# Six of sixteen gamma kv additions on VectorE, an identity run on TensorE ahead of the data, and a new hand-written order, in a gated recurrent layer kernel on one core

## The reference, cut to what matters

```python
xn = layernorm(x)
r, k, v = split(xn @ W_rkv + b_rkv)          # 128 wide each
r = sigmoid(r); k = exp(k); kv = k * v
# two scans over time, y[t] = lam * y[t-1] + u[t], lam = exp(-exp(nu_log)) per feature
u1 = scan(kv); u2 = scan(k)
gamma = exp(nu_log + gamma_log) - 1
s = ((u1 + gamma * kv) / (u2 + gamma * k + 1e-6) * r) @ W_o + b_o
# weights and xn are quantised in blocks of 32 to a 6 bit grid and back: xd, wd
g = silu(xd @ wd.T + bias)
out = x + s * g
```

## Time and profile before

| what | us |
|---|---|
| median of 3 runs | 125.94 (125.5 to 125.95) |
| the profiled execution, device time | 125.42 |
| its span in the trace | 123.6 |
| TensorE busy in the span | 109.6 (89%) |
| GpSimd busy | 106.4 (86%) |
| VectorE busy | 105.1 (85%) |
| ScalarE busy | 104.7 (85%) |
| TensorE weight loads, beside the matmuls | 58.5 (47%) |

### The profile page before, as it was taken

One profiled execution on the slowest core, in us unless ns is written; L12 is line 12 of the kernel. 1 busy time (PEld: TensorE's weight loads), 2 busy tenths in 40 slices (PEclk: granted clock), 3 DMA queues, 4 the chain that ended last, 5 costly groups with the idle time before them and its releaser, 6 DMA issues.

```text
span 123.6 us, 1670 instructions
## 1 busy us (share of the span) xinstructions
PE 109.6 (89%) x387; PEld 58.5 (47%) x387; DVE 105.1 (85%) x167; ACT 104.7 (85%) x180; POOL 106.4 (86%) x127
## 2 busy tenths in 40 slices
PE   0008989999999999999999999999999999999980
PEld 0006444444555555555455555544654655554450
DVE  0446999999998999999999948998969989993881
ACT  4047799999999999999969899999999979999800
POOL 2288699999997999999999999999999999998400
PEclk9999999999999999999999999999999999999999
DMA  2879930000020000110201020200102002012026
GB/s 66 248 237 402 386 127 0 0 3 0 0 90 5 0 0 26 59 58 27 85 0 65 25 85 0 85 0 3 72 15 90 0 3 85 31 54 85 0 85 255
DMA packets 6025, 8.82 MB, mean 71 GB/s; under 512 B 1536, under 2 KB 1920, under 8 KB 6016
## 3 DMA queue, kind: packets, MB, share of 16 engines
q1 hardware_dynamic: 5040, 8.72, 19.4%
q10 hardware_dynamic: 976, 0.00, 0.4%
HBM read 4.53 MB, written 4.19 MB: 71 GB/s over the span
## 4 chain that ended last, share of the span: by engine, by line
POOL 39%; ACT 17%; PE 16%; issue 12%; DVE 9%; DMA 3%; ACTq 1%; DVEq 1%; POOLq 0%
POOL den L302 8%; POOL mixed L308 7%; PE taken_ps L946 6%; POOL rstd L256 6%; POOL q L279 6%; ACT L679 4%; POOL xd L286 4%; PE v_ps L968 4%; POOL gk L296 3%; ACT den L744 3%; DMA x_all<-in_L_attn_inputs_dram 3%; PE turned_ps L925 3%; POOL xn L271 2%; ACT gate L739 2%; DVE kv L451 2%
## 5 line engine op out<-in xcount | busy, mean ns | idle before, releaser
L946 PE MATMUL taken_ps<-xnT,wrkv_sb 128*128 128x512 f32 x64 | 33.0, 611 | 0.3 <-ACT recept L731 0.3
L696 ACT ACTIVATE xn<-x_all,shift,rstd 128x128 f32<-128x128 f32 x48 | 19.8, 486 | 6.4 <-POOL shift L260 6.4
L308 POOL TENSOR_TENSOR mixed<-mixed,den 128x512 f32<-128x512 f32 x16 | 20.3, 1277 | 1.8 <-DVE mixed L478 1.7
L679 ACT ACT_TABLE_LOAD x16 | 20.5, 1283 | 1.0 <-PEq L1170 0.7
L302 POOL TENSOR_TENSOR den<-den,gk 128x512 f32<-128x512 f32 x16 | 20.4, 1279 | 1.0 <-DVE den L460 0.8
L469 DVE TENSOR_TENSOR_SCAN num_ps<-own_ps,kv 128x512 f32<-128x512 f32 x16 | 19.5, 1217 | 0.2
L460 DVE TENSOR_TENSOR_SCAN den<-own_ps,k 128x512 f32<-128x512 f32 x16 | 19.2, 1204 | 0.3 <-POOL mixed L308 0.3
L925 PE MATMUL turned_ps<-ident,xn 128*128 128x128 f32 x64 | 10.4, 292 | 9.6 <-POOL xn L271 9.6
L422 DVE BATCH_NORM_STATS2 stats<-x_all 128x6 f32<-128x256 f32 x32 | 11.8, 415 | 7.3 <-DMA x_all<-in_L_attn_inputs_dram 7.3
L279 POOL TENSOR_TENSOR q<-xn,inv_scale 128x512 fp8e4<-128x512 f32 x16 | 16.8, 1053 | 1.1 <-DVE inv_scale L443 1.1
L968 PE MATMUL v_ps<-xnT,wrkv_sb 128*128 128x512 f32 x32 | 17.2, 619 | 0.0
(11 more groups left out here) (62 smaller groups left out, 181.0 us busy)
## 6 DMA issues: line engine op xcount, KB each, us to landing
x_all<-in_L_attn_inputs_dram SPq DMA_DIRECT2D x16, 256.0 KB, 6.6
out_dram<-x_all SPq DMA_DIRECT2D x16, 256.0 KB, 2.0
wrkv_sb<-in_L_attn_W_rkv_dram SPq DMA_DIRECT2D x1, 192.0 KB, 4.4
wf_sb<-in_L_ffn_weight_dram SPq DMA_DIRECT2D x1, 64.0 KB, 6.4
wo_sb<-in_L_attn_W_o_dram SPq DMA_DIRECT2D x1, 64.0 KB, 6.1
cols<-in_L_attn_nu_log_dram ACTq DMA_DIRECT2D x1, 0.5 KB, 3.9
cols<-in_L_attn_gamma_log_dram ACTq DMA_DIRECT2D x1, 0.5 KB, 4.2
cols<-in_L_attn_b_o_dram ACTq DMA_DIRECT2D x1, 0.5 KB, 4.6
```

Of the source, the lines that this page charges most:

```text
L308: nc.gpsimd.tensor_tensor(mixed[:, n % MIX, :], mixed[:, n % MIX, :], den[:, n % DEN, :], ALU.mult)\
L679: act.add_instruction(mybir.InstLoadActFuncSet(name=nc.get_next_instruction_name(), engine=mybir.EngineType.Activation, act_func_set_id=n, ...
L696: ins = nc.scalar.activation(xn[:, n % XN, j * D:(j + 1) * D], x_all[:, n, j * D:(j + 1) * D], ACT.Identity, bias=shift[:, t:t + 1], scale ...
L946: nc.tensor.matmul(taken_ps[i % 2][:, :], weights, moving, start=True, stop=True).then_inc(filled, 1)
```

## The change

It has three parts.

1. For sequences 2, 5, 7, 9, 11 and 13, `gamma_kv(n)` goes from TensorE's list to VectorE's. There it is one SCALAR_TENSOR_TENSOR, num = kv * gamma + num, that reads and writes `num_ps`. The other ten stay on TensorE, `arm_num` too.
2. TensorE begins with `warm_up()`: 32 transposes of the identity into `v_ps`, which wait for the identity alone.
3. The lists of calls of GpSimd, VectorE, ScalarE and TensorE, and `TURNS` and `TAKEN` with them, stand in a new order. ScalarE has seven calls each of `exp_phase` and `silu_phase` in place of eight. SyncE's order of loads and stores is as before. GpSimd's calls are the same 103, in another order.

```diff
+    WARM_UP = 32
...
     TURNS = [
-        ("xn", 0), ("xn", 1), ("xn", 2), ("xn", 3), ("xd", 0), ("xd", 1), ("xn", 4), ("xn", 5), ("xn", 6),
+        ("xn", 0), ("xn", 1), ("xn", 2), ("xn", 3), ("xn", 4), ("xd", 0), ("xd", 1), ("xd", 2), ("xn", 5),
...
     TAKEN = [
-        ("k", 0), ("k", 1), ("r", 0), ("r", 1), ("k", 2), ("k", 3), ("r", 2), ("z", 0), ("r", 3), ("z", 1),
+        ("k", 0), ("k", 1), ("r", 0), ("r", 1), ("r", 2), ("k", 2), ("k", 3), ("k", 4), ("z", 0), ("r", 3),
...
             def scan_num(n):
                 if n == 0:
+                    dve.wait_ge(lam_placed, 1)
                     dve.wait_ge(num_armed, 1)
...
+            def gamma_kv(n):
+
+                dve.wait_ge(num_scanned, n + 1)
+                nc.vector.scalar_tensor_tensor(num_ps[:, :], kv[:, n % KS, :], gam[:, 0:1], num_ps[:, :],
+                                               ALU.mult, ALU.add).then_inc(num_done, 1)
...
+            def warm_up():
+
+                pe.wait_ge(ident_ready, 1)
+                for i in range(WARM_UP):
+                    nc.tensor.transpose(v_ps[:, 0:P], ident[:, :], ident[:, :])
...
+            warm_up()
             transpose_xn(0)
             transpose_xn(1)
             keys(0)
+            keys(1)
             values(0)
             arm_num()
-            keys(1)
```

More of the change, by code:

```diff
@@ L352, in _ @@
[L352 to L356, removed]
+            quantise(5)
+            denominator(4)
+            quantise(6)
+            normalise(9)
+            normalise(10)
+            quantise(7)
+            gamma_k(5)
+            dequantise(5)
+            gamma_k(6)
+            ratio(3)
+            inv_std(5)
+            normalise(11)
             dequantise(6)
-            normalise(10)
+            gamma_k(7)
@@ L563, in _ @@
+            scan_num(1)
+            statistics(9)
             scan_den(2)
-            scan_num(2)
             key_values(3)
-            statistics(9)
+            receive(1)
+            scan_den(3)
+            block_maxima(3)
+            statistics(10)
+            statistics(11)
+            statistics(12)
             gating(0)
-            receive(2)
-            block_maxima(3)
-            residual(0)
             block_scales(3)
             inverse_scales(3)
-            statistics(10)
+            key_values(4)
@@ L574, in _ @@
+            scan_num(2)
+            residual(0)
+            gamma_kv(2)
+            scan_den(4)
+            receive(2)
+            gating(1)
+            statistics(13)
             scan_num(3)
-            scan_den(3)
-            key_values(4)
+            residual(1)
+            block_maxima(4)
+            key_values(5)
             receive(3)
-            scan_num(4)
-            key_values(5)
-            statistics(11)
-            statistics(12)
-            block_maxima(4)
-            receive(4)
@@ L584, in _ @@
-            gating(1)
             block_scales(4)
             inverse_scales(4)
-            scan_num(5)
-            residual(1)
-            key_values(6)
-            statistics(13)
-            scan_den(4)
-            gating(2)
-            block_maxima(5)
-            scan_den(5)
-            residual(2)
+            scan_den(5)
+            scan_num(4)
+            gating(2)
+            statistics(14)
+            key_values(6)
+            residual(2)
+            receive(4)
+            statistics(15)
@@ L596, in _ @@
+            block_maxima(5)
+            scan_num(5)
+            block_scales(5)
+            inverse_scales(5)
+            gamma_kv(5)
+            key_values(7)
+            receive(5)
+            gating(3)
             scan_den(6)
-            receive(5)
-            statistics(14)
-            gating(3)
-            key_values(7)
             scan_num(6)
+            scan_den(7)
+            block_maxima(6)
             residual(3)
             key_values(8)
-            block_scales(5)
@@ L605, in _ @@
-            inverse_scales(5)
-            statistics(15)
-            receive(6)
-            scan_den(7)
-            gating(4)
-            scan_num(7)
-            key_values(9)
-            residual(4)
-            scan_den(8)
-            receive(7)
-            block_maxima(6)
-            gating(5)
-            scan_num(8)
             block_scales(6)
             inverse_scales(6)
-            residual(5)
-            gating(6)
-            receive(8)
-            key_values(10)
-            scan_num(9)
@@ L625, in _ @@
-            residual(6)
+            receive(6)
+            scan_num(7)
+            gamma_kv(7)
+            key_values(9)
+            receive(7)
+            gating(4)
+            scan_num(8)
+            residual(4)
+            key_values(10)
+            scan_den(8)
+            receive(8)
+            gating(5)
+            scan_num(9)
+            key_values(11)
+            residual(5)
+            gamma_kv(9)
             scan_den(9)
             receive(9)
+            gating(6)
             scan_num(10)
+            scan_den(10)
@@ L869, in _ @@
[L869 to L886 removed]
+            normalise(13)
+            copy_xdT(8)
@@ new lines, in _ @@
+            receptance(10)
+            normalise(14)
+            gates(7)
+            copy_xnT(12)
+            receptance(11)
+            copy_xnT(13)
+            receptance(12)
+            gates(8)
+            exp_phase()
+            logarithm(8)
+            logarithm(9)
+            keys(12)
+            keys(13)
+            logarithm(10)
+            inverse(8)
+            inverse(9)
+            copy_xdT(9)
+            inverse(10)
+            copy_xdT(10)
+            normalise(15)
@@ L910, in _ @@
             gates(13)
             exp_phase()
+            logarithm(14)
+            copy_xdT(15)
+            inverse(13)
+            inverse(14)
             logarithm(15)
```

443 lines of the change are left out of this document (201 added, 242 removed), and 14 rows, old and new, of tables (TAKEN, TURNS).

## The result

| | before | after |
|---|---|---|
| median us of 4 runs each, same chip | 125.72 (125.1 to 125.95) | 121.67 (121.62 to 121.83) |
| ratio, 95% interval | | 0.969 (0.965 to 0.973) |
| profiled execution, us | 125.42 | 121.62 |
| its span | 123.6 | 119.8 |
| first `quantise` starts | 13.53 | 12.51 |

The change is faster by 3.1%. The forecast was 123.9 with a range from 122.5: the direction was right and the size was not. Against the profiled execution it said -2.0 us; it is -3.8.

What follows compares the result with a forecast made beforehand. GpSimd was taken as the bound: start -0.7, waits that go -2.5, tail -0.2, new waits +1.0 and +0.4 gave -2.0, so 123.4 against the profiled 125.42; plus 0.5 for the runs' median, 123.9, range 122.5 to 125.7 plus 0.2.

Steps and rivals of the forecast that it cites:

- start of GpSimd's stretch: First `quantise`, behind VectorE's first reciprocal: starts at 12.86 in place of 13.53, -0.7 us.
- waits that go: GpSimd's waits ahead of the last `ratio` (1.69 us) and `denominator(3)` (0.85) vanish in the new order, -2.5 us.
- tail: Two ScalarE table loads fewer: the last `project` no longer waits 0.20 for the last `gates`, -0.2 us.
- Waits that come: +1.0 us found: `quantise(2)` on GpSimd: ready at 24.8 but waits for VectorE's third reciprocal, ending at 25.8, +1.0 us.
- +0.4 us assumed: GpSimd, middle of its stretch: small new waits not visible in the lists, +0.4 us, ends 0 and 2.2.
- rival 4: Lighter TensorE and ScalarE free everyone: no wait at `quantise(2)` or in the middle, -1.4 more, 122.5; chance 0.15.
- rival 2: New order gives back on GpSimd what it takes: new middle waits reach 2.2, +1.8, 125.7, no change; chance 0.14.
- TensorE: 5.2 us less, not on the path: Six products leave TensorE, 0.86 us each; nothing on GpSimd's list waits for TensorE directly, only VectorE's waits shorten.
- The warm up, worth 0: TensorE's start: early clock could bring `key_values(0)` forward, but VectorE's queue holds it to 15.3; 0 to 0.3 us, chosen 0.
- rival 3: TensorE's clock falls back while idling before data; `key_values(0)` and passes behind it come 0.6 later, up to 124.5; chance 0.15.
- just hidden: VectorE's six new passes, 0.66 us each, 4.0 in all, cost nothing if it idles at most 2.6 us before `receive(15)`.
- the -1.69: Last `ratio` on GpSimd: its 1.69 us wait for `receive(15)` goes because `receive(15)` and `gating(12)` change places.

Runs made afterwards that it cites:

- The 126.06: Changed kernel with the six gamma kv additions put back on TensorE, so all sixteen there, new order and warm up kept: 126.06 us, ratio 1.004.
- the 125.69: Changed kernel, additions left on VectorE, with six other TensorE products (receptance 5 and 8, keys 11, project 6, 8, 10) made twice: 125.69 us, ratio 1.001.
- the early `ffn_weights()`: Changed kernel without the warm up and with `ffn_weights()` moved ahead of `key_values(0)`: 122.11 us, ratio 0.971; with the warm up kept: 121.74, 0.969.

## Why the prediction was wrong in size

By its own steps, against the profiled 125.42:

| step | said | measured |
|---|---|---|
| start of GpSimd's stretch | -0.7 | -1.0 |
| waits that go | -2.5 | -2.5 |
| waits that come | +1.4 | -0.4 |
| tail | -0.2 | +0.2 |
| sum | -2.0 | -3.8 |
| median of the runs above the profiled execution | +0.5 | 0.05 |

(The third row is what is left of the -2.9 of GpSimd's stretch: 0.25 us fewer small waits, the rest in GpSimd's own passes. The measured rows add up to -3.8 before rounding.)

The last row is chance. The median of three stood 0.5 above the one execution that was profiled, and it makes up 0.45 of the 2.2 us between 123.9 and 121.67.

- **"Waits that come: +1.0 us found"** is the step that failed. It put the third reciprocal at 25.8; it ended at 24.35. It took VectorE's passes ahead of it to have the durations that they had before, and looked only at which of them were moved. But the five passes of `ffn_weights` took 1.3 us (17.71 to 19.00) in place of 2.45 (15.80 to 18.25), since they now stand beside the inverse square root. The rows that would have told it stood in the trace of before. VectorE in order of time:

```profile
16.11 0.62 DVE L515 TENSOR_SCALAR wscale<-wmax 128x4 f32<-128x4 f32 x1
...
17.31 1.02 DVE L523 TENSOR_TENSOR wd<-wq,wscale 128x128 f32<-128x128 fp8e4 x1
```

  and GpSimd beside it:

```profile
15.66 1.05 POOL L279 TENSOR_TENSOR q<-xn,inv_scale 128x512 fp8e4<-128x512 f32 x1
16.69 0.45 POOL L271 TENSOR_SCALAR xn<-x_all,rstd,shift 128x128 f32<-128x128 f32 x1
```

  `wscale`, 128 x 4 numbers, took 0.62 us and ended at 16.73, `quantise` at 16.71. `wos_sb` gave 0.4 back (0.44 before, 0.83 now, where it ends with a `dequantise`: 23.19 and 23.12). The remaining 0.7 of the 1.45 is partly that the fifth input tile landed 0.28 earlier (10.04 against 10.32); I have not taken it apart further.
- **"+0.4 us assumed"** for small waits in the middle: GpSimd's small waits are 1.1 us in all, where those that were not to go had been 2.21 - 0.85 = 1.36. The lighter TensorE is needed to keep new ones away, as the run with six products made twice shows. That is half of rival 4. Its other half, no wait at `quantise(2)`, came true by another cause: with TensorE's load back, `quantise(2)` does not wait either (24.90, behind a reciprocal that ends at 24.82). Rival 4 had 0.15 where it should have had most of rival 2's chance too.
- **"TensorE: 5.2 us less, not on the path"** was wrong as reasoning, though it had no number in the sum. Its record count tells what the busy time of 99.74 of 100.40 did not: 354 matmul records are 185 halves of products, at 0.43 us each by the earlier trace rows, and 169 transposes at 0.11 to 0.12 from one start to the next (four from 106.77 to the product at 107.20 in the changed kernel): 98 to 100 us of 100.4. After, 332 records, 167 and 165 of them: 90 to 92 of 95.4. TensorE was as full as GpSimd. With the six products, 12 halves or 5.2 us, it would have 95 to 97 of 95.4: the new list of GpSimd could not have been fed by it without a wait. The 126.06 and the 125.69 are what that cost at the places tried. "Nothing on GpSimd's list waits for TensorE directly" is not so in the program either, though no such wait shows.
- **"The warm up, worth 0"**: its speed was called rightly (`key_values(0)` at 14.96 against a forecast of 15.3, `values(0)` at 1.02 in place of 1.74), its worth not: 1.0 us (122.64 against 121.67). The 0.6 by which `key_values(0)` would be late was seen, under rival 3, but the other 0.7, VectorE's passes slipping under GpSimd's, was not; and without that slip the 0.6 costs nothing in GpSimd's stretch, as the early `ffn_weights()` shows. The cap that the Trainium skill sets (TensorE: Matmul & The Clock Gate, Part 1: below 1% of a typical span) holds with 0.8%, at its edge. In the old order the warm up gained nothing.
- **Rival 3**, the clock that falls back, took place in five of the twelve traces with a warm up, but not in that of the change, and its price of 0.6 us does not show: in the three of the five whose list puts `key_values(0)` where the change does, it comes 2.45 to 2.67 us behind the first `quantise` (2.46 in the change), and `quantise(2)` waits in none.
- **VectorE's six passes, "just hidden"**: right. 0.67 to 0.76 us each, mostly with an advance of 0.66; VectorE idled 2.50 us where 2.6 were allowed; leaving them out gains nothing, four more cost 2.3 us.
- **The start**: 0.35 earlier than said, 0.28 of it because the fifth input tile landed earlier. The first `quantise` came between 12.35 and 13.21 in the runs with the new start, and between 13.49 and 13.91 with the old one, so this is partly chance of one execution.
- **The tail**: the last `project` no longer waits for ScalarE, as said. But it starts 0.56 behind the end of the last `ratio` (112.94, 113.50) and not 0.38 (116.88, 117.26), as TensorE is still at the transposes of `untranspose` till then.
- **The reason for the -1.69** was half right. The swap of `receive(15)` and `gating(12)` alone gained nothing in the old order; by the trace of that run ScalarE's last `gates`, behind two table loads, were late too, which "Beside GpSimd, so 0 at the end, but -0.2" did not say. In the changed kernel one load stands there, ahead of the last two `gates`, and they end at 113.34, before `project(15)`. That this load is what makes the swap pay was not tried by itself.

## What to carry to other kernels

When several engines are busy for 85% to 90%, the engine with the fewest idle microseconds is not the only bound: count how long the others' instructions must take at their own advance, and ask if they could feed a bound that runs faster. Here two parts of a change, each worth nothing alone, were worth 4 us together, so a part's value is only that beside the others. And when passes are moved, their durations move with them: look in the trace for passes of one shape with two durations, and at what the neighbour was doing.

## What the runs showed of the hardware that I had not expected

- Some short VectorE passes with all operands in SBUF end only when the large GpSimd pass beside them has ended. `wscale` takes 0.17 us beside the inverse square root. Beside a `quantise` it took 0.39, 0.46, 0.62 and 0.90 in different kernels, and ended 0.02 or 0.03 us after the `quantise` each time. `wd` took 0.29 beside the inverse square root, 0.32 just behind it, and 1.02 beside a `quantise` or `dequantise`, with its end 0.14 or 0.15 after theirs; `wos_sb` took 0.21 to 1.18 and always ended 0.08 to 0.14 after GpSimd's pass. What GpSimd runs decides, not how long: its inverse square root (2.9 us) does not hold them like this.
- Not all passes in SBUF are held. `wmax` (TENSOR_REDUCE) takes 0.26 to 0.28 us beside either, the reciprocals 0.18 to 0.36 and each BATCH_NORM_STATS2 0.37 to 0.44. Nor are passes with an operand in PSUM: the new pass takes 0.67 to 0.76, `key_values` 0.65 to 0.75. The Trainium skill has the resource (GPSIMD Engine Reference, "1. Specifications": the SBUF interfaces are shared with VectorE, with contention for VectorE instructions with two SBUF inputs or in a two port mode). The traces agree for `wq` and `wd`, which have two SBUF inputs; whether `wscale` and `wos_sb` ran in such a mode no row shows. They add that a pass can be held for 0.7 to 1.0 us. That the port is the cause is inferred from which passes are held; no run took it apart further.
- 32 transposes of the identity brought TensorE to its upper level in all twelve traces with the warm up (the last of them start 0.11 us apart, the first 0.21). In five of the twelve it fell back to 1.2 GHz around the first real transposes, behind 1.65 to 2.00 us of idling. The granted clock in the records is 0.50 there, but 1.00 in the slow stretch at the start of the traces without a warm up, so the durations are the safer sign.
